# A graph layer with attention on one core: where denominators, reciprocals and divisions stand in the queues

## The reference

```python
h = jnp.maximum(_layernorm(x, axis=-1), 0.0)
q = jnp.einsum('c,bcn->bn', wq, h)
k = jnp.einsum('c,bcn->bn', wk, h)
scores = q[:, None, :] + k[:, :, None]
scores = jnp.where(scores > 0, scores, NEG_SLOPE * scores)
att = jax.nn.softmax(scores, axis=-1)
agg = jnp.einsum('bcn,bmn->bcm', h, att)
out = jnp.einsum('oc,bcm->bom', adj, agg) + bm[None, :, None]
return x + jax.nn.relu(out)
```

## Time and profile before

| | us |
|---|---|
| median of 3 runs | 2362.61 |
| lowest and highest | 2360.57, 2365.11 |
| span of the profiled execution | 2365.7 |
| PE busy | 2187.1 (92%) |
| DVE busy | 2015.0 (85%) |
| ACT busy | 1194.9 (51%) |
| POOL busy | 1072.0 (45%) |

### The profile page before, as it was taken

The page is one execution under the profiler, slowest core; times in us unless marked ns, Lnnn a source line. Parts: engine busy times, 40 slices in busy tenths (PEclk is TensorE's granted clock), DMA queues, the critical chain, the costliest instruction groups (busy, mean ns, idle before and its releaser), DMA issues.

```text
span 2365.7 us, 37878 instructions
## 1 busy us (share of the span) xinstructions
PE 2187.1 (92%) x12336; PEld 1039.0 (44%) x12336; DVE 2015.0 (85%) x3183; ACT 1194.9 (51%) x1905; POOL 1072.0 (45%) x714
## 2 busy tenths in 40 slices
PE   5999989989999999998999999999999999999999
PEld 2444444444444444444444444444444444444444
DVE  7889888898888888888978889888898888988886
ACT  4545545455544555454554545454455544555554
POOL 2444434445344444444444444444454444444444
PEclk9999999999999999999999999999999999999999
DMA  2211112101121011221111211111101121111100
GB/s 98 72 45 45 63 64 72 59 32 62 62 71 68 22 67 61 70 72 40 47 63 67 71 47 44 62 63 71 58 31 62 62 72 63 36 57 62 69 36 36
DMA packets 57838, 137.50 MB, mean 58 GB/s; under 512 B 7776, under 2 KB 7776, under 8 KB 57696
## 3 DMA queue, kind: packets, MB, share of 16 engines
q1 hardware_dynamic: 57696, 135.82, 16.5%
HBM read 68.69 MB, written 67.11 MB: 57 GB/s over the span
## 4 chain that ended last, share of the span: by engine, by line
DVE 41%; PE 32%; issue 16%; ACT 6%; POOL 3%; DVEq 1%; DMA 0%; ACTq 0%; SPq 0%; POOLq 0%
DVE p_lo L635 15%; DVE p L629 9%; PE acc L298 8%; PE acc L299 8%; PE acc L300 8%; DVE v_lo L653 4%; DVE stats L535 4%; ACT leak L396 3%; POOL psum_n L755 3%; PE small L256 2%; DVE b_ps L617 2%; DVE normed L667 2%; DVE a_ps L617 2%; PE vps L280 1%; DVE sum_lo L648 1%
## 5 line engine op out<-in xcount | busy, mean ns | idle before, releaser
L298 PE MATMUL acc<-p_hi,v_hi 128*128 128x512 f16 x2048 | 793.0, 387 | 11.8 <-issue 9.8
L299 PE MATMUL acc<-p_lo,v_hi 128*128 128x512 f16 x2048 | 793.4, 387 | 0.0
L300 PE MATMUL acc<-p_hi,v_lo 128*128 128x512 f16 x2048 | 792.3, 387 | 0.0
L760 POOL TENSOR_TENSOR res<-res,xs 128x512 f32<-128x512 f32 x256 | 455.4, 1779 | 627.0 <-ACT res L415 627.0
L755 POOL TENSOR_TENSOR psum_n<-psum_n,p 128x512 f32<-128x512 f32 x384 | 520.6, 1356 | 409.3 <-DVE p L629 392.6
L635 DVE SCALAR_TENSOR_TENSOR p_lo<-p,p_hi 128x512 f16<-128x512 f32 x512 | 665.5, 1338 | 0.3
L415 ACT ACTIVATE res<-normed,bias_o,unscale_o 128x512 f32<-128x512 f32 x256 | 207.9, 812 | 669.1 <-DVE normed L667 669.1
L629 DVE SCALAR_TENSOR_TENSOR p<-a_ps,A_col,leak 128x512 f32<-128x512 f32 x512 | 357.8, 738 | 45.4 <-ACT leak L396 45.4
L280 PE MATMUL vps<-wmT_hi,h_hi 128*128 128x512 f16 x1024 | 389.4, 380 | 4.1 <-DVE v_lo L653 1.8
L281 PE MATMUL vps<-wmT_lo,h_hi 128*128 128x512 f16 x1024 | 389.1, 380 | 0.0
L282 PE MATMUL vps<-wmT_hi,h_lo 128*128 128x512 f16 x1024 | 389.0, 380 | 0.0
(11 more groups left out here) (74 smaller groups left out, 1462.6 us busy)
## 6 DMA issues: line engine op xcount, KB each, us to landing
xs<-in_x_dram SPq DMA_DIRECT2D x128, 512.0 KB, 3.8
out_dram<-res SPq DMA_DIRECT2D x256, 256.0 KB, 2.1
xs<-in_adj_dram SPq DMA_DIRECT2D x1, 1024.0 KB, 9.6
res<-in_L_gnn_wq_dram SPq DMA_DIRECT2D x1, 256.0 KB, 6.2
res<-in_L_gnn_wk_dram SPq DMA_DIRECT2D x1, 256.0 KB, 7.4
wqk_col<-in_L_gnn_wq_dram SPq DMA_DIRECT2D x1, 2.0 KB, 6.4
wqk_col<-in_L_gnn_wk_dram SPq DMA_DIRECT2D x1, 2.0 KB, 7.7
bias_o<-in_L_gnn_bm_dram SPq DMA_DIRECT2D x1, 2.0 KB, 7.5
```

Of the source, the lines that this page charges most:

```text
L298: pe.matmul(ps[:, :], v_hi[:, nt, cols], p_hi[:, hf, nt, :], start=(nt == 0), stop=False)
L299: pe.matmul(ps[:, :], v_hi[:, nt, cols], p_lo[:, hf, nt, :], start=False, stop=False)
L300: mm = pe.matmul(ps[:, :], v_lo[:, nt, cols], p_hi[:, hf, nt, :], start=False, stop=(nt == NT - 1))
L760: pool.tensor_tensor(res[:, k, :], res[:, k, :], xs[:, b[1], ot, hf * HALF:(hf + 1) * HALF], ALU.add).then_inc(s_add, 1)
```

## The change

The queues of three engines change. On PE the denominator of the first half moves from step 3 to step 7 of unit 0, its spread from the end of unit 0 to step 5 of unit 1; the denominator of the second half from step 4 of unit 4 to the start of unit 5, its spread from the end of unit 4 to step 4 of unit 5. On DVE the division of units 0 to 2 moves behind the `p_lo` pair of its step, the first reciprocal from the first step to the second, and the second reciprocal behind the first `h_lo` of the next image. On ACT `rden` and the relus of units 0 to 2 move behind the work on numerators that they stood ahead of.

```diff
             def period(b, more):
-                unit(b, 0, {1: lambda: spread_z(b, 1), 3: lambda: denominator(b, 0)})
-                spread_reciprocal(b, 0)
-                for k in range(1, OT):
-                    unit(b, k)
-                unit(b, OT, {4: lambda: denominator(b, 1)})
-                spread_reciprocal(b, 1)
-                unit(b, OT + 1)
+                unit(b, 0, {1: lambda: spread_z(b, 1), 7: lambda: denominator(b, 0)})
+                unit(b, 1, {5: lambda: spread_reciprocal(b, 0)})
+                unit(b, 2)
+                unit(b, 3)
+                unit(b, OT)
+                unit(b, OT + 1, {0: lambda: denominator(b, 1), 4: lambda: spread_reciprocal(b, 1)})
                 unit(b, OT + 2)
...
                 leaks(b, NT + 2)
+                p_uppers(b, NT + 2)
                 copy_reciprocal(b, 0)
+                leaks(b, NT + 4)
                 relu(b, 0)
-                p_uppers(b, NT + 2)
-                leaks(b, NT + 4)
-                relu(b, 1)
                 p_uppers(b, NT + 4)
                 leaks(b, NT + 6)
+                relu(b, 1)
+                p_uppers(b, NT + 6)
                 relu(b, 2)
-                p_uppers(b, NT + 6)
                 sum_upper(b, 1)
...
                 for m in range(NT // 2):
 
-                    if m > 0:
-                        normalised(b, m - 1)
                     numerators(b, NT + 2 * m)
-                    if m == 0:
+                    if m == 1:
                         reciprocal(b, 0)
                     if more:
                         statistics(nxt(b), [m])
                     p_lowers(b, NT + 2 * m)
+                    if m > 0:
+                        normalised(b, m - 1)
                 sum_lower(b, 1)
                 if more:
                     normaliser(nxt(b))
                 normalised(b, 3)
+                if more:
+                    h_lower(nxt(b), [0])
                 reciprocal(b, 1)
                 if more:
-                    h_lower(nxt(b), [0, 1])
+                    h_lower(nxt(b), [1])
```

## The result

| | before | after |
|---|---|---|
| median, us | 2363.75 (2360.57 to 2365.11, 4 runs) | 2408.49 (2408.09 to 2408.90, 4 runs) |
| ratio, 95% interval | | 1.0192 (1.0177 to 1.0206) |
| span of the profiled execution | 2365.7 | 2406.7 |
| mean granted clock of PE | 0.978 | 0.994 |

The change makes the kernel 1.9% slower, by 45 us. The forecast was 2418, in a range of 2380 to 2452.

What follows compares the result with a forecast made beforehand. No engine bounds the whole span; DVE and PE lead by turns within an image. 0.58 + 1.27 = 1.85 us per image, times 32 is 59, less 4 for the clock, giving 2418 us, range 2380 to 2452.

Steps and rivals of the forecast that it cites:

- The third division and `sum_hi`, +0.55: Second half's numerators: the later third division delays relu and `sum_hi` on ACT, so `sum_lo` starts 0.55 us later per image.
- `sum_lo` meets `res`, +0.62: End of the numerators: POOL's `res` of the third unit starts just ahead of DVE's `sum_lo`, lengthening it by 0.62 us.
- Inside unit 5, +1.27: PE in unit 5: denominator 0.21, spread 0.49 and a 0.57 wait for the late reciprocal add 1.27 us per image.
- unit 5's start +0.58 in all: PE starts unit 5 0.58 us later: two terms totalling 1.17, less the reciprocal and spread no longer ahead of it.
- The first half's denominator and spread, 0: First half on PE: moving denominator, spread and reciprocal later costs 0, as PE has time to spare there.
- Waits of about 1.2 ahead of units 2, 3 and 4: PE waits for the later divisions, about 1.2 us ahead of each of units 2, 3 and 4.
- The sum, 1.85 per image: Whole image: 0.58 to unit 5's start plus 1.27 inside it, 1.85 us, times 32 images 59 us.
- a credit of 4 of 7 us: PE's low clock behind its long wait costs about 7 us in all; 4 of these credited as regained by the change.
- Milder: Rival: `sum_lo` meets no `res` and the reciprocal is ready in time, 0.66 us per image, 2380 us; chance 0.13.
- Low clock in unit 5: Rival: a slow-clock stretch over the start of unit 5 on PE costs 35 us more, 2453 us; chance 0.12.
- POOL waits the pair out: Rival: POOL does not get between the two `p_lo`, saving 1.07 us in each of two steps, 2350 us; chance 0.05.
- PE bounds: Rival: PE bounds after all, so its waits for the denominators, up to 82 us, are gained, 2280 us; chance 0.02.

Runs made afterwards that it cites:

- e12: Changed kernel with POOL's `res` of unit 2 held back until the whole normaliser chain is done: 2390.75 us, ratio 1.0118.
- e4: Changed kernel with POOL's `res` of unit 2 made to wait until the second half's `sum_lo` is done: 2413.44 us, ratio 1.021.
- e3: Changed kernel with ACT doing the second half's `sum_hi` ahead of the relu of unit 2: 2375.7 us, ratio 1.0052.
- e1: Changed kernel with the second half's denominator, spread and reciprocal put back, so only the first half's part of the change: 2387.68 us, ratio 1.0102.
- e11: Kernel before with only the second denominator, spread and reciprocal moved, plus 28 idle matmuls ahead of unit 5, before PE's wait: 2377.88 us, ratio 1.0064.
- e5: Kernel before with 18 idle matmuls on PE ahead of the second half's denominator: 2355.72 us, ratio 0.9969.
- e2: Kernel before with only the second half's denominator, spread and reciprocal moved as in the change: 2426.0 us, ratio 1.0266.
- e6: Kernel before with division 3 and the second reciprocal ahead of the normaliser on DVE, and the last division between `h_full` and `h_rest`: 2356.93 us, ratio 0.9975.
- e7: e6 with the second denominator and spread moved into unit 5, as the change has them: 2345.28 us, ratio 0.9916.

## Why the prediction was right, point by point

**No engine is the bound; follow one image.** Held. PE, DVE and POOL are all less busy after, and the kernel is slower.

**The third division and `sum_hi`, +0.55.** The mechanism held and every station of it is in the rows: the short `p_lo` pair, the one that meets half a sum, two of 3.22 that meet both, the divisions within 0.10 us of their forecast (the second to the digit by luck: the first came 0.10 late, and the step was 0.10 short). The size came out at +0.41 (22.68 to 23.09). I had taken 6.35 for a step; it is 6.25, and the way from the third division over relu and `sum_hi` to `sum_lo` is 2.08, not 2.13.

**`sum_lo` meets `res`, +0.62.** Held: 1.34 instead of 0.68, +0.66. e12 took it away alone and got back 0.67 per image, 17.7 us. The Trainium skill ("SBUF — State Buffer", section "SBUF: two separate sides") says that a GpSimd instruction and a VectorE one that has two SBUF inputs, or runs in a mode with two ports, shut each other out for the whole length of the one that started first. The rows agree for `sum_lo`, which has two SBUF inputs: it starts 0.48 behind `res` and ends 0.55 behind the end of `res`. They agree for `var_eps` too, which ends 0.02 (e4) and 0.03 (e3) behind `res`; it has one tensor input, and in what mode it ran no run shows.

**Inside unit 5, +1.27, and unit 5's start +0.58 in all.** Held. With the +0.55 taken off, they give +1.30 from `sum_lo` to a_ps; measured +1.36 (23.37 to 24.73), of which 0.66 is the first half's (e1) and 0.69 the second's (e11; worked out beforehand as 1.27 less the 0.59 for a reciprocal and spread no longer ahead of unit 5, 0.68). The wait for the reciprocal inside the unit was 0.34, not 0.57, but the spread came at 8.94, against 8.90 worked out, since PE reached it 0.3 later than I had it. Here the reciprocal leads, not PE, and so that error cost nothing.

**The first half's denominator and spread, 0.** Held as far as e1 can tell: its 1.04 per image over e5 is filled by the two terms above (0.66 and 0.37), and PE's wait of 1.08 for the first reciprocal came out of spare time.

**Waits of about 1.2 ahead of units 2, 3 and 4.** Held in kind, somewhat shorter: 1.20, 0.90, 0.97, and 1.58 ahead of unit 5.

**The sum, 1.85 per image.** Measured against e5, in which the clock lengthens hardly any image either: 1.74 in the images in the middle (73.42 from `sum_lo` to `sum_lo`, where I had named 73.5 as the sign). On 32 images the difference is 3.5 us. The whole is 2408.5 less 2355.7, 52.8 us, and 54.7 without the 2.0 us that the idle matmuls cost e5 in its last image. 32 times 1.74 would be 55.7. The 0.9 between comes from the ends. I had taken the last image like the others, but from its `sum_lo` on it is 0.1 us shorter after than before, not 1.7 longer. The first `sum_lo` comes 0.4 sooner than in e5, and the interval that ends at the last `sum_lo` is longer by 3.0, 1.2 over the 1.74.

**The clock, a credit of 4 of 7 us.** Mis-sized. The low clock cost the kernel before 8.9 us, and hardly any of it is on the path after, so 8.9 was due, 4.9 more than I credited. I had worked out 7 myself and kept back 3 with no row behind it. The 7 itself was near by luck: I read it from the profiled execution, which is slower than the median, and there it was 13.8 us (2365.7 less 2353.9, and the 2.0). I had counted the stretch of double length two times, and the first and the last of the 31 images from one `sum_lo` to the next have it as well, with 1.8 and 1.9 us. The three items, 3.5, 0.9 and 4.9, are the 9.3 us between 2417.8 (2418 unrounded) and 2408.5.

**The rivals.** "Milder" fell: `sum_lo` did meet `res`, and the spread came as late as forecast. "Low clock in unit 5" did not come in the kernel after, for the reason that stood against it, that its waits are short; e2 shows that it comes at once when the same wait is in one piece. I had put the waits ahead of units 2 to 4 down as evidence for this rival. They are what prevents it: e2 without them has the low clock, the kernel after has not. The price I gave this rival, 2453, lies 1 us outside the range that was to take it in. "POOL waits the pair out" fell: both late `p_lo` pairs took 3.22. (Its saving of 1.07 in each of two steps is 2.14, not 2.12; nothing hangs on it.) "PE bounds" fell, with the second wait right behind the first.

## What to carry to other kernels

Before moving an instruction away from a wait, look for the second wait behind it, and work out in a table when each division, sum and reciprocal comes: such a forward working was right within 0.15 us over 23 us here. A long wait of PE in one piece cost twice in e2, once in waiting and once in the clock behind it. So judge an order with its waits filled by idle matmuls: e2 and e6 looked far worse than the orders in them were. Take off what the idle matmuls cost where there is no wait to fill, as in the last image here. And when two engines hold each other up as DVE and POOL do here, ask where the other's instruction lands after any edit, small operations included.

## What the runs showed of the hardware that was not expected

- A DVE `tensor_scalar` on 128 x 4 elements is held up by a running POOL addition as the large `sum_lo` is: `var_eps` took 0.99 (e4), 1.24 (e3) and 1.10 us (e7) instead of 0.17. In e4 the `BATCH_NORM_AGGREGATE` group ahead of it was not lengthened.
- After a wait of 4.05 us of PE in one piece the granted clock was 0.50 for the next 5 us (e2); with the same wait filled by unused matmuls it was 1.00 (e11). In e7 no wait in the 9 us before is longer than 0.9 us, and the clock falls in some images and not in others with the same instructions (a_ps at 21.8 or 23.4). What decides there stays open.
- Doing more matmuls made the kernel faster: 18 idle ones per image took 35 us off e6.
